# Unread products on TensorE from the program's begin, and values' products beside the rotated queries

## The reference

```
layer 0: relu linear attention, 8 heads of 32; feed-forward with a ternary weight (round(weight / mean|weight|))
layer 1: latents kv_d and q_d of 64 channels; keys and queries of 16 heads, each half plain (k1, q1)
         and half rotated (kr from x, qr from q_d); values v = Wv_u kv_d + bv_u; softmax attention;
         feed-forward: 16 experts that choose tokens by a softmax over router logits
layer 2: attention with decaying running sums; gated feed-forward with ternary weights, rms norm
layer 3: state space attention with a convolution; gated feed-forward with ternary weights
```

## Time and profile before

| | us |
|---|---|
| median of 3 runs (lowest, highest) | 1033.42 (1028.28, 1034.17) |
| profiled execution, its span | 1029.84, 1028.0 |
| PE busy | 946.4 (92%) |
| PEld, DVE busy | 481.0 (47%), 715.1 (70%) |
| ACT, POOL busy | 464.8 (45%), 435.2 (42%) |

### The profile page before, as it was taken

The page is one execution under the profiler, slowest core; times in us unless marked ns, Lnnn a source line. Parts: engine busy times, 40 slices in busy tenths (PEclk is TensorE's granted clock), DMA queues, the critical chain, the costliest instruction groups (busy, mean ns, idle before and its releaser), DMA issues. The chain is left out here.

```text
span 1028.0 us, 12619 instructions
## 1 busy us (share of the span) xinstructions
PE 946.4 (92%) x4494; PEld 481.0 (47%) x4498; DVE 715.1 (70%) x1327; ACT 464.8 (45%) x767; POOL 435.2 (42%) x444
## 2 busy tenths in 40 slices
PE   4999799879999999878999997999999999999997
PEld 2677555323333333344555646633662474256325
DVE  3777565678888888547777773768586777758674
ACT  2333045247766666645575451621371246134411
POOL 2222357554444333017245361087128505840770
PEclk9999799979999999998999997999999999999999
DMA  8700035312211220030000001000000000000000
GB/s 295 259 16 16 16 105 141 123 40 65 63 47 49 63 63 2 1 146 1 17 16 1 16 1 44 1 0 1 21 1 1 1 21 1 0 1 22 0 1 21
DMA packets 28942, 43.67 MB, mean 42 GB/s; under 512 B 6512, under 2 KB 22080, under 8 KB 28480
## 3 DMA queue, kind: packets, MB, share of 16 engines
q1 hardware_dynamic: 28880, 42.87, 13.4%
HBM read 31.38 MB, written 11.27 MB: 41 GB/s over the span
## 5 line engine op out<-in xcount | busy, mean ns | idle before, releaser
L2180 POOL TENSOR_TENSOR l_scaled<-l_X,l_source 128x512 f32<-128x512 f32 x112 | 135.6, 1240 | 141.6 <-ACT l_X L2250 124.6
L1102 DVE TENSOR_REDUCE l_nmax<-banks 128x1 f32<-128x512 f32 (+1 forms) x165 | 147.7, 929 | 34.9 <-PE banks L1211 33.7
L1057 ACT ACTIVATE l1b_PT<-banks 128x512 f32<-128x512 f32 (+1 forms) x176 | 134.1, 793 | 66.8 <-PE banks L1224 66.4
L1211 PE MATMUL banks<-l_KQ 96*128 96x512 bf16 x240 | 81.3, 392 | 8.6 <-DVE l_nmax L1102 5.8
L1224 PE MATMUL banks<-l_KQ 99*128 99x512 bf16 x256 | 85.0, 385 | 3.0 <-ACT l1b_PT L1057 2.1
L2263 ACT ACTIVATE l_hhi<-l_h 128x512 f16<-128x512 f32 (+1 forms) x24 | 15.1, 630 | 129.4 <-DVE l_h L2375 129.4
L2599 PE MATMUL banks<-l_scaled,l_cbm 128*64 128x512 f32 x224 | 59.5, 613 | 10.7 <-POOL l_scaled L2180 10.6
L1238 PE MATMUL banks<-l1b_PT,l1b_V 128*32 128x512 f32 x512 | 68.2, 605 | 0.0
L2349 DVE TENSOR_TENSOR l_decayed<-banks,l_right_decay 128x512 f32<-128x512 f32 x56 | 38.4, 686 | 37.9 <-PE banks L2599 37.9
L2621 PE MATMUL banks<-l_decayed,w_place 64*128 64x512 f32 x224 | 63.2, 641 | 0.0
L1783 PE MATMUL banks<-l_xhi,l_ternary 128*128 128x512 f16 x128 | 49.8, 389 | 8.6 <-DVE l_h L1713 8.6
(11 more groups left out here) (342 smaller groups left out, 2052.1 us busy)
## 6 DMA issues: line engine op xcount, KB each, us to landing
l_split<-l1a_parts SPq DMA_DIRECT2D x16, 384.0 KB, 3.3
l_KQ<-l_split SPq DMA_DIRECT2D x48, 128.0 KB, 2.9
l_KQ<-l_split SPq DMA_DIRECT2D x16, 192.0 KB, 3.1
l_KQ<-l_split SPq DMA_DIRECT2D x48, 64.0 KB, 2.8
w_ternary<-l_tern_out SPq DMA_DIRECT2D x7, 384.0 KB, 2.3
x<-in_x SPq DMA_DIRECT2D x4, 512.0 KB, 9.4
l_raw<-in_w_gate_up SPq DMA_DIRECT2D x2, 1024.0 KB, 9.9
out<-x SPq DMA_DIRECT2D x4, 512.0 KB, 3.0
```

What stands on the lines that cost most here:

```text
L1057: nc.scalar.activation(PT[:, first:first + size, :], source, ACT.Exp, scale=SCALE).then_inc(p_ready, 1)
L1102: nc.vector.tensor_reduce(nmax[:, H % 2, first:first + size], source, axis=AX.X, op=ALU.max, negate=True).then_inc(smax_read, 1)
L1211: last = nc.tensor.matmul(ps[bank + m][:, :], KQ[pairs, QUERY, g, j, t * P:(t + 1) * P], KQ[pairs, KEY, g, j, :], start=True, stop=True)
L2180: nc.gpsimd.tensor_tensor(by_head(scaled[:, (2 * u + m) % 4, :]), by_head(X[:, T, :]), spread(source[:, level, T, :]), ALU.mult).then_inc( ...
```

## The change

Five edits. (1) The block ahead of layer 0 goes; its three memsets stand at the begin of POOL's program in layer 0. (2) x of batch 0 is loaded in two transfers with a semaphore each, and the statistics of its tiles 0 and 1 wait only for the first. (3) A helper keep_going issues fp32 matmuls whose results are never read: 26 of 128 columns at PE's begin in layer 0 (after the memset of ones), 3 of 512 columns before the last turn of layer 0, 2 before the last turn of layer 1, 3 at the end of layer 2. (4) In project1 the values' products move: two after each rotated-query product, into ps[6] and ps[1], and DVE reads them in two pieces of 512 columns ahead of the expert results. (5) The expert products go in pairs into ps[2] and ps[3]; four reads of DVE by half banks become two of a whole one.

```diff
-def norm_stats(k, dve, own, xb, stats, mv, var_eps, var_ready):
+def norm_stats(k, dve, own, xb, stats, mv, var_eps, var_ready, arrivals={}):
     for t in range(TT):
+        if t in arrivals:
+            dve.wait_ge(arrivals[t], 16)
         last = nc.vector.bn_stats(stats[:, t, :], xb(t))
...
+def keep_going(k, bank, rhs, times, weights=None):
+    for _ in range(times):
+        k.nc.tensor.matmul(bank, (weights or k.ident)[:, :], rhs, start=True, stop=True)
...
+            nc.gpsimd.memset(k.ones[:, :], 1.0).then_inc(k.constants_set, 1)
+            nc.gpsimd.memset(k.minus_half[:, :], -0.5).then_inc(k.constants_set, 1)
+            nc.gpsimd.memset(k.xn[:, :, :], 0.0).then_inc(k.constants_set, 1)
+            pool.wait_ge(k.constants_set, 3)
             invert(0)
...
-                else:
-                    dve.wait_ge(k.x0_loaded, 16)
-                norm_stats(k, dve, own, lambda t: k.x[:, b % B, t, :], stats, mv, rstd, var_ready)
+                norm_stats(k, dve, own, lambda t: k.x[:, b % B, t, :], stats, mv, rstd, var_ready,
+                           arrivals={0: k.x0_loaded, 2: k.x0_rest_loaded} if b == 0 else {})
...
+            pe.wait_ge(k.constants_set, 1)
+            keep_going(k, ps[2][:, 0:P], k.ones[:, :], 26, k.ones)
             pe.wait_ge(*k.groups["small"])
             turn_input(0)
...
+            keep_going(k, ps[turn_banks(B - 1)[0]][:, :], w.qkv[:, 0, 0:S], 3)
             turn_attended(B - 1)
             project(B - 1)
...
+    V_BANKS = (6, 1)
...
-                for t in range(TT):
-                    dve.wait_ge(y_made, b * TT + (t + 1))
-                    nc.vector.tensor_tensor(y0[:, b, t, :], ps[2 + t][:, 0:C], w.rows[:, E_ROW, :], ALU.add)
-                    nc.vector.tensor_tensor(values[:, b, t, :], ps[2 + t][:, C:2 * C], w.rows[:, V_ROW, :],
-                                            ALU.add).then_inc(y_read, 1)
+                for half in range(2):
+                    dve.wait_ge(v_made, b * 2 + (half + 1))
+                    nc.vector.tensor_tensor(values[:, b, 2 * half:2 * half + 2, :], halves(ps[V_BANKS[half]][:, :]),
+                                            w.rows[:, V_ROW, :].unsqueeze(1).broadcast_to([P, 2, C]), ALU.add).then_inc(v_read, 1)
+                for half in range(2):
+                    dve.wait_ge(y_made, b * 2 + (half + 1))
+                    nc.vector.tensor_tensor(y0[:, b, 2 * half:2 * half + 2, :], halves(ps[2 + half][:, :]),
+                                            w.rows[:, E_ROW, :].unsqueeze(1).broadcast_to([P, 2, C]), ALU.add).then_inc(y_read, 1)
...
                     pe.wait_ge(lmax_ready, b)
+                    pe.wait_ge(v_read, b * 2)
...
                     pe.wait_ge(lmax_ready, B)
+                    pe.wait_ge(v_read, B * 2)
...
                     pe.wait_ge(lat_ready, B)
+                    pe.wait_ge(v_read, B * 2 - 1)
...
-                    pe.wait_ge(y_read, b * TT)
+                    pe.wait_ge(y_read, b * 2)
...
-                nc.tensor.matmul(ps[4][:, :], w.up[HI, P:2 * P], latT[HI, :], start=True, stop=True).then_inc(qr_made, 1)
-                nc.tensor.matmul(ps[5][:, :], w.up[HI, 2 * P:3 * P], latT[HI, :], start=True, stop=True).then_inc(qr_made, 1)
-
-                for t, (ready, value) in enumerate(((k1_ready, b + 1), (q1_ready, b + 1), (qrot_done, b * 2 + 1),
-                                                    (qrot_done, b * 2 + 2))):
+                if b:
+                    pe.wait_ge(qrot_done, b * 2)
+                pe.wait_ge(lmax_ready, b + 1)
+                for turned in range(2):
+                    nc.tensor.matmul(ps[4 + turned][:, :], w.up[HI, (1 + turned) * P:(2 + turned) * P], latT[HI, :],
+                                     start=True, stop=True).then_inc(qr_made, 1)
+                    for t in (2 * turned, 2 * turned + 1):
+                        last = nc.tensor.matmul(ps[V_BANKS[turned]][:, t % 2 * C:(t % 2 + 1) * C], latT[LO, t * P:(t + 1) * P],
+                                                w.up[LO, P:3 * P], start=True, stop=True)
+                    last.then_inc(v_made, 1)
+
+                for t, (ready, value) in enumerate(((k1_ready, b + 1), (k1_ready, b + 1), (q1_ready, b + 1), (q1_ready, b + 1))):
                     pe.wait_ge(ready, value)
-                    product(ps[2 + t][:, 0:C], lambda c: xnT[:, c, t * P:(t + 1) * P], lambda c: w.expert[:, c, :])
-                    nc.tensor.matmul(ps[2 + t][:, C:2 * C], latT[LO, t * P:(t + 1) * P], w.up[LO, P:3 * P],
-                                     start=True, stop=True).then_inc(y_made, 1)
+                    last = product(ps[2 + t // 2][:, t % 2 * C:(t % 2 + 1) * C], lambda c: xnT[:, c, t * P:(t + 1) * P],
+                                   lambda c: w.expert[:, c, :])
+                    if t % 2:
+                        last.then_inc(y_made, 1)
...
             turn_output(HEAD_GROUPS - 1)
+            keep_going(k, ps[KEY_BANK][:, :], w.rope[:, 0, :], 2)
             pe.wait_ge(attn_ready, HEAD_GROUPS)
...
                 sum_squares(b)
+            keep_going(k, ps[0][:, :], w.qkv[:, 0, 0:S], 3)
             pe.wait_ge(x_done, B * TT)
...
-            sp.dma_start(k.x[:, 0, :, :], x_in[:, 0]).then_inc(k.x0_loaded, 16)
+            sp.dma_start(k.x[:, 0, 0:2, :], x_in[:, 0, 0:2]).then_inc(k.x0_loaded, 16)
+            sp.dma_start(k.x[:, 0, 2:4, :], x_in[:, 0, 2:4]).then_inc(k.x0_rest_loaded, 16)
...
-        consts = k.sem("constants_set")
-        with nc.Block() as block:
-            @block.gpsimd
-            def _(pool):
-                nc.gpsimd.memset(k.ones[:, :], 1.0).then_inc(consts, 1)
-                nc.gpsimd.memset(k.minus_half[:, :], -0.5).then_inc(consts, 1)
-                nc.gpsimd.memset(k.x[:, B, :, :], 0.0).then_inc(consts, 1)
-                pool.wait_ge(consts, 3)
+        k.constants_set = k.sem("constants_set")
```

More of the change, by code:

```diff
@@ L627, in project1 @@
         y_read = sem("y_read")
+        v_made = sem("v_made")
+        v_read = sem("v_read")
         lmax_ready = sem("lmax_ready")
@@ L864, in _ @@
                 first_scores(i)
-            pe.wait_ge(y_read, B * TT)
+            pe.wait_ge(y_read, B * 2)
             pe.wait_ge(early.smax_read, PAIRS)
@@ L2700, in program @@
         k.x0_loaded = k.sem("x0_loaded")
+        k.x0_rest_loaded = k.sem("x0_rest_loaded")
         k.x_loaded = k.sem("x_loaded")
@@ L2738, in _ @@
                     sp.wait_ge(k.x0_loaded, 16)
+                    sp.wait_ge(k.x0_rest_loaded, 16)
         weight_scopes[0].close()
```

## The result

| | before | after |
|---|---|---|
| median of 7 runs, us | 1034.17 | 1026.08 |
| spread, us | 1028.28 to 1034.54 | 1022.19 to 1027.66 |
| profiled execution, us | 1029.84 | 1027.12 |
| its span, us | 1028.0 | 1025.3 |

A forecast was written before the change was run, and what follows sets the result against it. TensorE, busy for 92% of the span, was taken as the bound. Terms 0 + 3.0 - 4.0 + 2.0 + 2.4 + 5.0 = 8.4 us off 1029.84 gave 1021.4, called 1021.5; range 1017 to 1027, with rivals 1012 to 1033.

The forecast's parts named there:

- Layer 3's start, +5.0 forecast: Layer 3's first transposes and two matmul groups run at the upper clock after three unread products: gain 5.0 us.
- The rival on the fillers: Fillers fail to hold the clock at the ends of layers 1 and 2; layer 1-2 border falls: 1030, chance 0.18.
- if layer 3 still starts at 0.50: Stated sign of being wrong: granted clock still at 0.50 when layer 3 begins, where 5.0 us were forecast.
- Layer 1's transitions and last batch, -2.0 forecast: Layer 1's three batch changes lose 4.0 us (0.4 gained each, less clock falls); after the last batch 2.0 are gained.
- Two falls in three, as forecast: Likeliest in layer 1: the clock falls in two of three new waits of some 2.5 us, costing 2.6 each.
- The slower rival: Clock stays down long after falls at the start and in all three batches, 5.0 us each: 1036, chance 0.08.
- The last store, 0 forecast: Kernel's end: the sum has no term for the last store; the table lists the rest with it as 0.
- The start, 0 forecast: Ternary weights' products start 2.9 us sooner, but a clock fall in 2.6 us of new idling takes 2.9 back.
- The end of layer 0, +3.0: Three unread products hold the clock through 2.69 us of idling; last transposes and projection run faster: gain 3.0 us.
- The uneven pair: Layer 1: half-as-long values' products beside query products; by program-order ends, saving nearer 1.6 than 2.5 us a batch.
- The rival "no overlap": Layer 1's values' products don't overlap the queries', so TensorE has no new idling there: about 1019.5, chance 0.07.
- The rival that the clock holds everywhere: Clock also holds in the new idle times at the start and in layer 1, +2.9 + 5.2: 1013.4, chance 0.25.

The follow-up runs named there:

- the start alone: Kernel before plus only: no first block, x in two loads, 26 unread products: 1028.19 us, 0.9963; its second kernel omits the 26: 1027.07 us, 0.9967.
- the last one without the 26 products: Changed kernel with unread products in every new idle time, borders and layer 2's first gates, but without the 26 at the begin: 1012.56 us, 0.9812.
- the fillers alone: Kernel before plus only the unread products at the ends of layers 0, 1 and 2 (3, 2 and 3): 1022.35 us, 0.9899.
- the last two kernels: Changed kernel with new idle times, borders and layer 2's first gates filled, with the 26 products (1009.14 us) and without them (1012.56 us).
- the start without the 26 products: Kernel before plus only the removed first block and x in two loads, no 26 unread products: 1027.07 us, 0.9967.
- the best kernel: Changed kernel with unread products in every new idle time, borders and layer 2's first gates, keeping the 26: 1009.14 us, 0.9777.

## Why the prediction was right in sign and wrong in size, and which step failed

The sign held, and most of the mechanism: the time falls, what is won comes from the clock at the ends of layers, and what is lost goes to the clock in layer 1. The size was off by 5.7 us in the profiled execution (8.4 forecast, 2.7 found); three terms are to blame (4.0, 2.0 and 2.2), two smaller ones miss by 0.7 each, and 3.9 us of unforecast gains stand against them.

*Layer 3's start, +5.0 forecast, +1.0 found: the step that failed most.* I argued that 1.7 us of idling are "less than any idle time after which the clock fell". That compared idle times one by one. After the fillers 1.56 us are open ahead of the transposes and 1.38 behind them, with 1.07 of work between, and the clock fell. The rival on the fillers named this pair ("short idle times follow the transposes") and got 0.18, too little for this place. The fall came at 629.0, so that the prediction's sign of being wrong, "if layer 3 still starts at 0.50", was met for all but the transposes. The kernel with both sides filled took 14.6 for 17.94 us, so the cause, idling around the transposes, is shown; which of the two idle times would have been enough isn't, since no run fills one alone. In two other executions with the same pair (layer 1's waits filled with four products or two) the clock was down for 3.4 us, not 6.8, and the stretch took 16.3. At the end of layer 1 the same concern didn't come true (0.50 and 1.33 open, clock 1.00).

*Layer 1's transitions and last batch, -2.0 forecast, -4.0 found.* The mechanism is the one told: the latent product waits for ScalarE's copy, so PE's saving becomes idling. Both sizes were too small. The idle time was 3.5, not 2.5 us, since more left PE's queue than the values' 2.5 us: the expert products in pairs take 1.8 to 2.0 us for two tiles in one run, and from one batch's keys to the next one's transposes the queue is 3.1 us shorter. All three waits lost the clock in after's trace, not two, and the last for 8 us and more. With the waits filled the stretch is 4.4 us shorter (3.2 forecast without falls), 0.5 at each transition and 3.0 at the last batch (0.4 and 2.0 forecast); the falls cost 8.5 (5.2 forecast). Two falls in three, as forecast, came in another execution (layer 3's start filled) and cost 3.4. The slower rival's price of 5.0 a fall was right for one fall of three; its condition, that the work between the holes doesn't bring the clock back, wasn't met in the others.

*The last store, 0 forecast, -2.2 found.* From its issue to the span's end it took 6.3 us for 4.1:

```profile
L2174 SPq DMA_DIRECT2D out<-x x4: 372/380/389, 730.0 to 1019.0; - x4
...
DMA to landing us min/median/max: 3.0/3.3/5.1
```

No edit touches it. From its issue to the span's end went 4.1 to 4.2 us in eight of the thirteen profiled executions, 4.7 and 4.8 in the two kernels with the start alone, and 5.9 to 6.3 in three (after, the one with project1 as before, and the last one without the 26 products). The three kernels with the old start all have 4.1, but so have five of the ten with the new one, each from one execution. The cause stays open.

*The start, 0 forecast, +1.0 found.* Gain 2.8 (2.9), idle 3.08 (2.6), and the fall cost the sixteen passes 1.8 us where I booked 2.9.

*The end of layer 0, +3.0 and +2.3.* The filled groups came as said; what was left out is what comes late next. With the projection sooner, the border's idle time ends with the ternary weights' store, issued at 111.74, and is 0.5 longer: layer 1 starts 3.44 us after that issue in after and in the fillers alone, 5.41 after it in before.

*The uneven pair.* The trace shows that passes of 256 columns start beside a pass of 512 and follow each other at 0.21 us while those start every 0.43 (147.07 to 148.36 above); four query passes with all eight values' passes take 1.8 us, what the query passes need alone. The Trainium skill (TensorE: Matmul & The Clock Gate, Part 3) states that matmuls start and end in program order, and by that rule the pairs should have cost 0.9 us a batch. It isn't borne out for these products: the second values' product of a pair starts at 147.50, halfway through its query product, and nothing was lost. The ends of matmuls in a trace are modelled, so this rests on the starts. The rival "no overlap" falls as well.

*The rival that the clock holds everywhere* was false of the change and is what filling makes nearly true: 1013.4 by its sum, 1009.1 with the borders filled too, where two falls are left (at 190 and 596 us).

*A slip.* The rival "no overlap" writes its time as 1021.4 + 4.0 - 2.0; these are the signs of gains. As a time it is 1021.4 - 4.0 + 2.0 = 1019.4, as the text then says.

*What the sum can't hold.* Layer 2 and the begin of layer 1, which no edit touches, gave +1.7 and +1.2 here. The prediction looked for falls at the six places of the diff only; before's trace has two more inside layer 2, from 463.6 for 6.8 us and from 613.8 for 3.4, after's has one of 3.4 (from 465.1). At layer 1's begin the time up to batch 0's keys runs from 9.1 to 15.4 us over the thirteen executions, though only the last two kernels edit anything there. The runs of the kernel before come in two groups, near 1029 and near 1034; with the borders and first gates filled as well, five runs lie within 2.3 us. That the two groups are short idle times that fall or don't is argued from this, not shown. The mean granted clock of the runs bears it out in part: in the start without the 26 products eight runs of 1026.2 to 1027.7 us have 0.972 to 0.975 and four of 1031.6 to 1032.8 have 0.967 to 0.969. A step of 0.006 is some 12 us more at half the clock, 6 us of time if all of it is matmuls, and that is the gap between them. Of the kernel before the upper group has 0.966 to 0.968 and the lower 0.968 to 0.973, which explains only about half of its 5 us.

## What to carry to other kernels

On a kernel that TensorE bounds, time taken off its queue ahead of a wait that another engine sets is no gain, and can be a loss: ask how long TensorE will idle there and what the clock does behind it. Look at idle times in groups: two of 1.6 and 1.4 us with a microsecond of work between cost up to nearly as much as one of 4.2 (16.3 to 17.9 and 19.0 us for a stretch of 14.6). Don't read a threshold out of one trace: the same idle time fell in one execution and held in the next. Fill such waits with products that nobody reads, up to where the awaited work arrives and no further: too few leave the fall (3 us at layer 3), too many hold the real work up (2.6 us at the start of the last kernel).

## What the runs showed that I had not expected

- The same idle time isn't always followed by a fall. 3.58 us ahead of batch 1's latent product lost the clock in after and kept it in the kernel with only layer 3's start filled; 0.44 and 0.78 us in layer 2 kept it in after and lost it in the best kernel. 1.87 us ahead of a latent product kept it, 1.56 and 1.38 on both sides of a microsecond's work lost it.
- A fall has no fixed price. In after's layer 1 the first two cost 1.7 us each and the third 5.1, about half of the 3.4, 3.4 and 10.2 us for which the granted clock was down. The whole time at the lower clock was 57 us in after's profiled run, 65 before, 24 in the best kernel.
- In all kernels the clock is down for 17 or 20.5 us at about 200 us, where the first scores go at VectorE's pace; filling wasn't tried there.
- Unread products in waits cost nothing that could be measured on the engines beside them: the best kernel has 25 such products more than after, 50 passes (its trace has 118 passes of unread products, after's 68), at the same busy times of VectorE (715.5 and 714.5), ScalarE (464.8 and 464.9) and POOL (435.3 and 434.6).
